# Convolution in plain fp32 on unsplit data, with one PSUM bank per group, magnitudes taken early, and a floor column

## What is computed

```
out = conv_general_dilated(x, weight, padding=[(4, 4)], feature_group_count=4)   # 9 taps, 4 groups of channels
out = out + einsum('nd,od->no', c, c_weight)[:, :, None] + bias[None, :, None]   # the context
...
x_scale = 448 / max(amax(|x2|), 1e-12);  w_scale likewise
x_fp8 = clip(x2 * x_scale, -448, 448).astype(float8_e4m3fn);  w_fp8 likewise
out = matmul(x_fp8, w_fp8.T) / (x_scale * w_scale)
x = x + out
```

## Time and profile before

| | us |
|---|---|
| median of 3 timed runs | 421.11 (420.65 to 422.22) |
| profiled execution | 420.53 |
| its span | 418.7 |
| TensorE busy | 406.2 |
| VectorE busy | 253.4 |
| ScalarE busy | 185.3 |
| GpSimd busy | 100.5 |

### The profile page before, as it was taken

How to read it: one execution, slowest core, us unless ns; L and a number is a source line. 1 busy time by engine, 2 the same in 40 slices (tenths; PEclk the granted TensorE clock), 3 DMA queues, 4 the chain that set the end, 5 groups by cost and what they waited for, 6 DMA issues and landing times.

```text
span 418.7 us, 5271 instructions
## 1 busy us (share of the span) xinstructions
PE 406.2 (97%) x1977; PEld 318.5 (76%) x1977; DVE 253.4 (61%) x393; ACT 185.3 (44%) x317; POOL 100.5 (24%) x81
## 2 busy tenths in 40 slices
PE   8999999999999999999999999998999999996896
PEld 4777787788888767888887788877869899996342
DVE  3658989446566633647666146577962533444994
ACT  6436796123565521346655113565641121111752
POOL 1002243152134322412523153134230222000000
PEclk9899999999999999999999999999999999999799
DMA  7994562512001000210100015001017373550036
GB/s 236 255 330 155 191 225 75 200 52 102 0 1 52 0 0 2 101 52 1 50 2 0 0 52 177 26 0 50 3 53 199 100 213 103 173 167 0 28 147 228
DMA packets 33258, 39.77 MB, mean 95 GB/s; under 512 B 2232, under 2 KB 20168, under 8 KB 33104
## 3 DMA queue, kind: packets, MB, share of 16 engines
q1 hardware_dynamic: 33056, 38.63, 28.5%
q0 software_dynamic: 176, 0.79, 0.5%
HBM read 26.12 MB, written 13.30 MB: 94 GB/s over the span
## 4 chain that ended last, share of the span: by engine, by line
PE 92%; DVE 3%; ACT 2%; issue 1%; POOL 0%; DVEq 0%; ACTq 0%
PE ps L536 36%; PE ps L521 19%; PE ps L567 11%; PE ps L519 5%; PE ps L546 4%; PE ps L481 4%; PE ps L674 4%; PE ps L662 3%; PE ps L597 2%; PE ps L442 2%; PE ps L571 1%; PE ps L495 1%; PE ps L464 1%; ACT a_buf L821 1%; PE ps L621 0%
## 5 line engine op out<-in xcount | busy, mean ns | idle before, releaser
L893 POOL TENSOR_TENSOR h_lo<-a_buf,h_hi 128x512 fp32r<-128x512 f32 (+1 forms) x44 | 57.5, 1307 | 139.1 <-ACT h_hi L776 139.1
L536 PE MATMUL ps<-x_hi,gate_w 128*128 128x512 f32 (+1 forms) x176 | 69.8, 397 | 0.1
L536 PE MATMUL ps<-x_hi,up_w 128*128 128x512 f32 (+1 forms) x176 | 69.7, 396 | 0.1
L536 PE MATMUL ps<-x_lo,gate_w 128*128 128x512 f32 (+1 forms) x176 | 69.5, 395 | 0.0
L521 PE MATMUL ps<-down_w,h_hi 128*128 128x512 f32 (+1 forms) x176 | 69.4, 394 | 0.0
L521 PE MATMUL ps<-down_w,h_lo 128*128 128x512 f32 (+1 forms) x176 | 69.4, 394 | 0.0
L536 PE MATMUL ps<-x_lo,up_w 128*128 128x512 f32 (+1 forms) x176 | 69.3, 394 | 0.0
L1140 DVE TENSOR_TENSOR a_buf<-a_buf,b_buf 128x512 f32<-128x512 f32 (+1 forms) x44 | 52.4, 1190 | 13.7 <-ACT a_buf L821 12.1
L1137 DVE TENSOR_TENSOR b_buf<-ps,b_buf 128x512 f32<-128x512 f32 (+1 forms) x44 | 30.2, 686 | 19.9 <-ACT b_buf L808 15.6
L805 ACT ACTIVATE a_buf<-ps,gate_sc 128x512 f32<-128x512 f32 (+1 forms) x44 | 30.2, 686 | 25.9 <-POOL h_lo L893 23.6
L808 ACT ACTIVATE b_buf<-ps,up_sc 128x512 f32<-128x512 f32 (+1 forms) x44 | 30.1, 685 | 24.9 <-PE ps L536 24.8
(11 more groups left out here) (158 smaller groups left out, 587.7 us busy)
## 6 DMA issues: line engine op xcount, KB each, us to landing
turned<-stage SPq DMA_DIRECT2D x16, 512.0 KB, 2.9
x_nat<-in_x SPq DMA_DIRECT2D x4, 1024.0 KB, 6.7
xt<-turned SPq DMA_DIRECT2D x8, 512.0 KB, 4.2
out<-o_buf SPq DMA_DIRECT2D x7, 512.0 KB, 2.9
x_nat<-in_down_q SPq DMA_DIRECT2D x11, 256.0 KB, 3.0
x_nat<-in_gate_q SPq DMA_DIRECT2D x10, 256.0 KB, 5.7
x_nat<-in_up_q SPq DMA_DIRECT2D x10, 256.0 KB, 7.1
x_hi<-turned SPq DMA_DIRECT2D x4, 512.0 KB, 4.0
```

Source lines behind the costliest of these rows:

```text
L536: last = mm(ps[0:k, bank(ic, 2 * m), :], w[:, H * ic + c * k:H * ic + (c + 1) * k], part[:, c, :], start=c == 0 and part is x1_hi, stop=c ...
L893: nc.gpsimd.tensor_tensor(h_lo[0:k, ic, :], a_buf[0:k, ic % 2, :], plain(h_hi[0:k, ic, :]), ALU.subtract).then_inc(h_lo_ready, 1)
```

## The change

The convolution reads x2 and its weights as plain fp32, without a high and a low part. So there are half as many matmuls in the code, of 128 columns, a group fills one bank, and four banks take turns. ScalarE's and GpSimd's splitting of x2 and of the weights goes; stores and loads move half the bytes, and there are eight xt buffers instead of four. VectorE reduces each group straight from PSUM, then ScalarE evicts it to t_t. ScalarE takes unscaled magnitudes into t16 during the last eight groups, and VectorE's round_from multiplies by the scale. The floor of the two maxima is a constant column set at the start, not an instruction. o_buf has three slots in use instead of four. The order of loads and stores on SyncE is written anew.

```diff
-OUTS = 4
+OUTS = 3
 WARM = (4, 2, 1, 6, 1)
 LRC = R * I // P
 MIX_BANK, BIAS_BANK = 5, 4
 FIRST_BANK = (6, 3, 7, MIX_BANK)
 EARLY = 6
-XT = 4
+XT = 8
...
+CONV_BANKS = 4
 CONV_AFTER = (3, 3, 2, 8)
+LATE = GROUPS - TG
+LOADS = ((8, 11), (11, 13), (13, 14), (14, 15))
...
-        conv_wt = sb("conv_wt", [P, SHIFTS, 2, P], F32R)
+        conv_wt = sb("conv_wt", [P, SHIFTS, P], F32)
...
-            sp.dma_start(stage_conv[:].rearrange("p s n -> p (s n)"), conv_w).then_inc(conv_in, 16)
+            sp.dma_start(conv_wt[:].rearrange("p s n -> p (s n)"), conv_w).then_inc(conv_in, 16)
...
             def store(g):
-                sp.wait_ge(stage_hi_ready, g + 1)
-                sp.wait_ge(stage_lo_ready, g + 1)
-                sp.dma_start(turned[g].rearrange("m p h -> p m h"), plain(stage[:])).then_inc(stored, 16)
+                if g == GROUPS - 1:
+                    sp.wait_ge(x2_last, 1)
+                else:
+                    sp.wait_ge(x2_ready, g + 1)
+                sp.dma_start(turned[g], x_nat[:, g, :]).then_inc(stored if g < LATE else stored_late[g - LATE], 16)
 
             def load(g):
-                sp.wait_ge(stored, 16 * (g + 1))
+                if g < LATE:
+                    sp.wait_ge(stored, 16 * LATE)
+                else:
+                    sp.wait_ge(stored_late[g - LATE], 16)
                 if g < XT:
                     sp.wait_ge(q_mm, 2 * TILES * IC)
                     sp.wait_ge(xt_zero, XT)
                 else:
                     sp.wait_ge(conv_mm, g - XT + 1)
-                sp.dma_start(plain(xt[g % XT][:, :, 1:P + 1]),
-                             turned[g].rearrange("m (b c) (k n) -> (c k) (m b) n", b=GB, n=P)
+                sp.dma_start(xt[g % XT][:, :, 1:P + 1],
+                             turned[g].rearrange("(b c) (k n) -> (c k) b n", b=GB, n=P)
...
             for g in range(XT):
                 load(g)
             for j in range(TG):
-                for g in range(CONV_FROM[j] + XT, min(CONV_FROM[j] + CONV_AFTER[j] + XT, GROUPS)):
-                    if j == TG - 1 and g == GROUPS - 3:
-                        store(GROUPS - 1)
+                for g in range(*LOADS[j]):
                     load(g)
-                if j < TG - 1:
-                    store((TILES - 1) * TG + j)
+                store(LATE + j)
+            for g in range(LOADS[-1][1], GROUPS):
+                load(g)
...
-                    pe.wait_ge(conv_ready, 1)
+                    pe.wait_ge(conv_in, 16)
                     pe.wait_ge(ctx_ready, 2)
                     pe.wait_ge(u_ready, TILES * IC)
-                if g >= 2:
-                    pe.wait_ge(z_ready, g - 1)
+                if g >= CONV_BANKS:
+                    pe.wait_ge(z_ready, g - CONV_BANKS + 1)
+                to = ps[:, g % CONV_BANKS, :]
                 for b in range(GB):
-                    bank_out = ps[:, 2 * (g % 2) + b // 2, :].rearrange("p (b n) -> p b n", b=2)
                     for k in range(SHIFTS):
-                        for m in range(2):
-                            mm(bank_out[:, b % 2, :], xt[g % XT][:, m * GB + b, k:k + P],
-                               conv_wt[:, k].rearrange("p m n -> p (m n)"),
-                               start=b % 2 == 0 and k == 0 and m == 0, stop=False)
-                    if b % 2 == 1:
-                        last = mm(bank_out[:, :, 0:P].rearrange("p b (f o) -> p b f o", f=PHASES),
-                                  ctx_pick[:, g:g + 1].to_broadcast([P, P]),
-                                  ctx_rhs[:, b - 1:b + 1].unsqueeze(2).to_broadcast([P, 2, PHASES, S]),
-                                  start=False, stop=True)
-                last.then_inc(conv_mm, 1)
+                        mm(to[:, b * P:(b + 1) * P], xt[g % XT][:, b, k:k + P], conv_wt[:, k],
+                           start=b == 0 and k == 0, stop=False)
+                mm(to.rearrange("p (b f o) -> p b f o", b=GB, f=PHASES), ctx_pick[:, g:g + 1].to_broadcast([P, P]),
+                   ctx_rhs[:].unsqueeze(2).to_broadcast([P, GB, PHASES, S]),
+                   start=False, stop=True).then_inc(conv_mm, 1)
...
-            pe.wait_ge(x2_ready, GROUPS)
+            pe.wait_ge(x2_ready, GROUPS - 1)
+            pe.wait_ge(x2_last, 1)
+            pe.wait_ge(z_ready, GROUPS)
...
-                activation(conv_wt[:, :, 0, :], stage_conv[:], copy).then_inc(conv_hi, 1)
...
-            def stage_high(g):
-                act.wait_ge(x2_ready, g + 1)
-                if g > 0:
-                    act.wait_ge(stored, 16 * g)
-                activation(stage[:, 0, :], x_nat[:, g, :], copy).then_inc(stage_hi_ready, 1)
-
-            def conv_low(g):
+            def magnitude(g):
+
+                act.wait_ge(z_ready, g + 1)
+                if g == 0:
+                    act.wait_ge(down_mm, GROUPS)
+                    act.wait_ge(pd_mm, TILES)
+                activation(t16[:, :, g * P:(g + 1) * P], t_t[:, :, g * P:(g + 1) * P], ACT.Abs).then_inc(v_ready, 1)
+
+            def conv_evict(g):
 
                 act.wait_ge(conv_mm, g + 1)
+                act.wait_ge(amax_ready, g + 1)
                 if g == 0:
-                    act.wait_ge(h_ready, TILES * IC)
-                if g >= 2:
-                    act.wait_ge(z_ready, g - 1)
-                activation(conv_part[:, g % 2, :].rearrange("p (b n) -> p b n", b=GB), conv_out(g, 1),
-                           copy).then_inc(part_out, 1)
+                    act.wait_ge(q_mm, 2 * TILES * IC)
+                activation(t_t[:, :, g * P:(g + 1) * P].rearrange("p f (b o) -> p b f o", b=GB),
+                           ps[:, g % CONV_BANKS, :].rearrange("p (b f o) -> p b f o", b=GB, f=PHASES),
+                           copy).then_inc(z_ready, 1)
...
                         for g in range(first + before, end):
-                            conv_low(g)
-
-            def magnitude(n, g, k):
-
-                if n >= 2:
-                    act.wait_ge(m_ready, n - 1)
-                activation(by_chunk(v16[:, n % 2], k), t_t[:, :, g * P:(g + k) * P], ACT.Abs,
-                           scale=x_round).then_inc(v_ready, 1)
+                            conv_evict(g)
+                            if j == TG - 1:
+                                for n in range(2 * (g - first) - 1, 2 * (g - first) + 1):
+                                    if n >= 0:
+                                        magnitude(n)
...
-            act.wait_ge(x_scale_ready, 1)
+            magnitude(GROUPS - 1)
+            act.wait_ge(x_scale_ready, 4)
             for n, step in enumerate(steps):
-                if n == 4:
-                    act.wait_ge(x_scale_ready, 4)
-                if n >= 4:
-                    evict(n - 4, *steps[n - 4])
-                magnitude(n, *step)
-            for n in range(len(steps) - 4, len(steps)):
-                evict(n, *steps[n])
+                evict(n, *step)
...
-            def stage_low(g):
-                pool.wait_ge(stage_hi_ready, g + 1)
-                nc.gpsimd.tensor_tensor(stage[:, 1, :], x_nat[:, g, :], plain(stage[:, 0, :]),
-                                        ALU.subtract).then_inc(stage_lo_ready, 1)
...
+            for floor in (X_MAX, W_ALL - 1):
+                v.memset(amax[:, floor:floor + 1], AMAX_MIN).then_inc(floor_set, 1)
...
-                v.tensor_scalar(largest, largest, AMAX_MIN, None, ALU.max).then_inc(steps_done, 1)
+                v.reciprocal(inverse, largest).then_inc(steps_done, 1)
...
-                dve.wait_ge(part_out, g + 1)
-                if g == 0:
-                    dve.wait_ge(q_mm, 2 * TILES * IC)
-                v.tensor_tensor(t_t[:, :, g * P:(g + 1) * P].rearrange("p f (b o) -> p b f o", b=GB),
-                                conv_out(g, 0).rearrange("p b (f o) -> p b f o", f=PHASES),
-                                conv_part[:, g % 2, :].rearrange("p (b f o) -> p b f o", b=GB, f=PHASES),
-                                ALU.add).then_inc(z_ready, 1)
-                dve.wait_ge(z_ready, g + 1)
-                v.tensor_reduce(amax[:, PHASES * g:PHASES * (g + 1)], t_t[:, :, g * P:(g + 1) * P], AX_X, ALU.max,
+                dve.wait_ge(conv_mm, g + 1)
+                v.tensor_reduce(amax[:, g:g + 1], ps[:, g % CONV_BANKS, :], AX_X, ALU.max,
                                 apply_absolute_value=True).then_inc(amax_ready, 1)
...
-                            last = v.memset(plain(xt[n][:, :, at:at + 1]), 0.0)
+                            last = v.memset(xt[n][:, :, at:at + 1], 0.0)
...
-            v.tensor_tensor(x_nat[:, n, :], y_buf[:, n % 2, :], x_nat[:, n, :], ALU.add).then_inc(x2_ready, 1)
-            dve.wait_ge(stage_hi_ready, n + 1)
-            v.tensor_tensor(stage[:, 1, :], x_nat[:, n, :], plain(stage[:, 0, :]),
-                            ALU.subtract).then_inc(stage_lo_ready, 1)
+            v.tensor_tensor(x_nat[:, n, :], y_buf[:, n % 2, :], x_nat[:, n, :], ALU.add).then_inc(x2_last, 1)
...
```

(43 more changed lines are left out.)

39 lines of the change are left out of this document (14 added, 25 removed).

## The result

| | before | after |
|---|---|---|
| median of 8 runs each, taken in turns on one chip | 421.59 us (420.65 to 422.54) | 418.72 us (417.64 to 420.02) |
| profiled execution | 420.53 | 418.99 |
| its span | 418.7 | 417.2 |

The ratio is 0.993, with a 95% interval from 0.9909 to 0.995: the change takes 2.9 us, 0.7%, off the time. That is past the 419.0 that the prediction named for faster, by little: the interval ends at half a per cent. 1.1 of this is the size of the gain (4.0 expected, 2.9 measured). The other 0.5 is the kernel before, whose median was 421.59 in these runs and not the 421.11 that the sum started from.

A forecast was written before the change was run, and what follows sets the result against it. TensorE was taken to bound the kernel. From the profiled 420.53 us, 2.5 for the convolution and 1.6 for the tail came off, 0.07 for memsets was added: 416.5, plus 0.58 to the median, 417.1; range 415.0 to 419.4.

The forecast's parts named there:

- What bounds the kernel: Whole kernel: TensorE, busy 97% of the span; edits pay in its instructions, the 5.4 us tail, or its few waits.
- The convolution on TensorE: Convolution groups: plain fp32 takes 2.91 us per group instead of 3.07, 2.5 us less over 16 groups.
- Rival (a): Convolution: it does not get shorter, a plain record costing 0.118 us; 419.6 us in all; chance 0.07.
- rival (c): Convolution: TensorE's clock falls inside it under plain fp32; 458 us if in all 16 groups; chance 0.04.
- The tail: After the last convolution: copy, sum and floor instruction go and the maximum gets shorter, 1.60 us less.
- The covered wait for the 16 evictions: Tail: it ends about 1.4 us after the last convolution while the scales need over 3; cost nothing.
- Magnitudes: ScalarE's passes move from output stage to last eight convolution groups, worth 0; VectorE's scaled rounding stays at 0.42 us per 1024.
- Rival (b): Output stage: VectorE becomes its bound because rounding takes 1.22 us per 1024; +4.1, 421.2 us; chance 0.07.
- Copies, stores, loads: Splitting of x2 and weights, SyncE's transfers and the 1.1 us wait in the last tile: all costed at 0.
- the 0.07 of the two memsets: Opening: two more memsets ahead of the warm-up data add 0.07 us, at most 0.13.
- Three output buffers: Output stage: groups 13 and 14 wait for the store of groups 7 and 8; margin 1.1 us, cost 0.
- The clock: After the tail: TensorE's fall to half clock may be avoided (-1.2 us) or cover more matmuls (+1.0); taken as 0.

The follow-up runs named there:

- e1: The changed kernel run again with no edit: 418.17 us, ratio 0.9925 to the kernel before.
- e4: The changed kernel with four output buffers instead of three, m16 moved into free space: 418.79 us, ratio 0.9932.
- e5: The changed kernel with 24 redundant waits (12 more instructions) on VectorE in the last tile: 417.77 us, ratio 0.992.
- e6: The kernel before with 236 redundant waits (118 more instructions) on VectorE in the last three tiles: 422.68 us, ratio 1.0017.
- e10: Repeat of the changed kernel with both dummy matmuls in TensorE's idle places and 12 more VectorE instructions: 416.47 us, ratio 0.9885.
- e11: Repeat of the kernel before with dummy matmuls in TensorE's idle places in the tail: 419.88 us, ratio 0.996.
- e3: The kernel before with 11, 8 and 4 dummy matmuls in TensorE's idle places in the tail: 420.19 us, ratio 0.9958.
- e7: The changed kernel with both dummy matmuls in TensorE's idle places and 12 more VectorE instructions, first time: 416.39 us, ratio 0.9876.
- e8: The changed kernel with one old tail link back, ScalarE evicting each group before VectorE reduces it: 418.79 us, ratio 0.9939.
- e9: Repeat of the changed kernel with dummy matmuls in TensorE's idle places in the tail, no list change: 417.53 us, ratio 0.9907.
- e2: The changed kernel with 5, 7 and 4 dummy matmuls in TensorE's idle places in the tail: 417.34 us, ratio 0.9894.

## Why the prediction was right, and what it missed

**What bounds the kernel** holds. TensorE stands in nearly every piece of the chain after, and both parts of the change that shortened its path paid in full.

**The convolution on TensorE.** 2.5 expected, 2.53 found, the same in all nine profiles of the change. The conditioning rows gave the price: 24 records in 2.68. Columns alone, or the rule of four passes from the Trainium skill (FP8 and Floating Point Precision, TensorE Precision Notes), would have given nothing. The trace decides against that reading: the columns are equal, but the old form lay 0.118 apart and the plain one 0.1116. Rival (a) is out, and rival (c) too: the clock was at 1.00 through the whole convolution.

**The tail.** 1.60 expected, 1.59 found at equal clock, and 1.89 in the first pair of profiles, where the spread before had run at half clock (0.80 against 0.49); that 0.3 is the clock and not the change. The covered wait for the 16 evictions stayed covered.

**Magnitudes.** On ScalarE 0 was right: three of them are left behind the last convolution, beside the scales. The timeline of VectorE in the output stage answers to the earlier trace rows:

```profile
388.07 0.48 DVE L1174 TENSOR_SCALAR m<-t,small 128x1024 bf16<-128x1024 bf16 x1
```

The rounding takes 0.48 instead of 0.42 per 1024, and 0.35 instead of 0.29 for 512. Rival (b) was far off, so the Trainium skill (VectorE: DVE Perf Modes, What auto-detection actually checks), which lists no scalar operand among the conditions of the fast mode, agrees with the trace. The new form has a second operation, takes the scale from a column and reads t16 in four pieces instead of v16 in one; no run tells which of these makes the 0.06. The slack hid it in the first pair, where TensorE ran its first input addition at half clock. With the clock held, the first products wait for VectorE, whose way to them holds two roundings and is 0.08 longer, and each of the next two steps is 0.06 longer (1.87 against 1.81), just what one rounding has grown by. That makes up the 0.20. So the prediction's 0 for the rounding was wrong by 0.2 us at the held clock: it looked for slack at the last product, and there is none at the first ones.

**Copies, stores, loads.** 0 was right for the path. The turned stores land in 2.0 us. TensorE's waits still have the 1.1 us in the last tile:

```profile
PE ps L546 <- DVE small L1032: 1.1, 1, 1.1
```

The opening is where one profile told little. Up to the first convolution, four profiles of the kernel before and its variants took 317.5 to 318.6, nine of the kernel after and its variants 317.4 to 318.8. It is again the clock: the first conditioning took 6.37 after and 5.26 with four output buffers, at the same place of the program. The window from 17 to 18 us of these two profiles (length; busy of each engine; PEclk; DMA share; GB/s) shows it, and the earlier trace rows has it before:

```profile
17.00:18.00 1.00, 1.00 (x7) 1.00 (x7) 0.65 (x2) 0.07 (x1) 0.00 (x0) 0.50 0.51 99
```

```profile
17.00:18.00 1.00, 1.00 (x11) 1.00 (x11) 0.97 (x2) 0.30 (x2) 0.00 (x0) 1.00 0.61 116
```

The means are 318.0 and 318.2, and the clock accounts for that. In the opening it was at 0.50 for either 3.4 or 6.8 us. With 3.4, three profiles of the kernel before have 317.5 to 318.0 and three of the kernel after (e1, e4, e5) 317.4 to 318.0, both 317.8 in the mean; with 6.8, one of before (e6) has 318.6 and six of after 318.2 to 318.8. So the 0.07 of the two memsets can't be seen, and the 0.8 of the first pair is the clock's but for a tenth or so, 3.4 us low before and 6.8 after. It can also account for e10 being only 3.4 below e11, while the four later stretches differ by -2.53 - 1.59 + 0.20 + 0.17 = -3.75. In runs with a mean granted clock of 0.994 or more the kernels with TensorE kept busy have medians of 419.29 before (e3, e11) and 415.57 with the packet moved (e7, e10), in the others 420.45 and 416.55: 3.7 and 3.9 apart. Ten of the 21 runs before were of the faster kind and three of the eleven after. Whether the change makes the longer low stretch more frequent is not settled.

**Three output buffers.** 0, as expected.

**The clock.** In the first pair it fell 2.6 us behind the last convolution in both, so with the shorter tail more of the matmuls lay under it. The output stage took 0.81 more than at the held clock before (26.51 against 25.70) and 1.59 more after (27.49 against 25.90), so 0.78 of its 0.98 is the clock, not far from the upper bound of the prediction's step. But this too differs from one execution to the next: in the seven profiles with TensorE left idle it fell 2.1 (e8) to 5.0 us (e5) behind the last convolution, and in e1 and e5 it stayed low for 3.4 us instead of 6.8. So 0 with a range was right, and the forecast's bound has the right size. At a window shortly behind the tail, after:

```profile
386.00:387.00 1.00, 1.00 (x2) 0.00 (x0) 1.00 (x3) 0.00 (x0) 0.00 (x0) 0.50 0.00 0
```

**The term that was missing.** The forecast came true, but its sum has a gap that made the gain too large: it took the end, from the last eviction to the end of the span, as unchanged and had no term for it. It was 1.1 us longer in every profile of the change that left VectorE's list as it was. The prediction looked at every engine and at every transfer of data, and not at the packets that carry the instructions, though the page before has them in queues of their own. The price is not one of the new convolution or of its precision. It comes from a list of instructions that is ten shorter and so fetches its last piece at the worst moment; the kernel before takes it too, if its list is 118 longer. With this term, -4.0 + 1.1 = -2.9, which is the measured gain; that it fits to the digit is in part luck, since the 0.2 of the rounding is missing and the clock in the opening and behind the tail moves single executions by up to 1 us each.

The version that has the change and neither loss, e7 and e10, takes 416.4 us, 1.2% less than the kernel before.

## What to carry to other kernels

Price a matmul by the spacing of the same form and shape in the trace, not by its columns: here equal columns differed by 0.16 us in 3.07, over 16 groups 2.5 us. Behind the last convolution, count links of the chain; here each one that was taken off paid its full distance. And when an edit changes the number of an engine's instructions, look at the last microseconds for an instruction packet under the last store: with the clock held, twelve more instructions that do nothing made this kernel a microsecond faster (e9, e10). Without that, the clock's scatter hid it in the time (e5).

## What the runs showed of the hardware

- An 8 KB instruction packet that starts during the last store (256 KB) makes it land in 3.4 to 3.5 us instead of 2.4 to 2.5, and the program end about 1.0 us later. It was so in seven profiles (after, e1, e2, e4, e6, e8, e9) and in none of the six without it (before, e3, e5, e7, e10, e11). In all seven, fifteen of the 16 parts in which the store reports its end came as usual and one came 0.90 to 1.07 us behind them; in the other six the last came 0.01 to 0.03 behind. The packet itself took 0.31 us, and between 1 and 13 data packets of 2 KB started behind it. With a single one (e4, e8) the last part was 1.07 behind the others, with 13 (e9) 0.90. Why so small a packet costs a whole microsecond is not settled.
- The place of that packet goes by the count of VectorE's instructions: it started when 575 (577 in e5, e7 and e10) had begun in lists of 576, 586 and 588, and at 703 in the list of 704.
- Plain fp32 matmuls of 128 columns, two records each, ran at 0.1116 us per record in the convolution as in the conditioning, against 0.118 for one reduced-fp32 matmul of 256 columns.
- The bf16 rounding took 0.48 us for 1024 elements with a multiplication by a per-partition column in it and its input in four pieces, 0.06 more than without both.
- With TensorE kept busy through the tail its granted clock stayed at 1.00 until the last matmul in all six profiles, and this was worth 0.8 to 1.7 us. Left idle, it fell to 0.50 between 2.1 and 5.0 us behind the last convolution, for 3.4 or 6.8 us.
